# A four-layer graph network: the edges sorted by source in two lists, one gathered by pointers, one scattered as rows, and two heads added by TensorE

## What is computed

```python
# layer 0, per edge, two heads of 32
e     = sum(leaky_relu(fs[src] + fd[dst]) * attn);   alpha = softmax of e over edges with the same dst
x    += (h + sum over heads and edges of dst: softmax(fs[src] * r * alpha)) @ W1 + b1
# layer 1
x    += sum over edges of dst: h[src]
# layer 2
x    += h_self + sum over edges of dst: tensor product of h[src] with an MLP of the edge
# layer 3, four heads: here the sum runs over the edges of the SAME SRC
e     = leaky_relu(a_src[src] + a_dst[dst] + b);     att = softmax of e over edges with the same src
x    += mean over heads: sum over edges of src: att * (h @ w)[dst]
```

## Time and profile before

| | |
|---|---|
| median of 3 runs | 10985.76 us |
| the profiled execution | 10983.5 us, its span 10981.7 us |
| PE busy | 3477.1 us (32%) |
| DVE busy | 6501.1 us (59%) |
| ACT busy | 3250.7 us (30%) |
| POOL busy | 8117.5 us (74%) |
| DMA | 681.55 MB, 62 GB/s over the span |

### The profile page before, as it was taken

One profiled execution on the slowest core, in us unless ns is written; L12 is line 12 of the kernel. 1 busy time (PEld: TensorE's weight loads), 2 busy tenths in 40 slices (PEclk: granted clock), 3 DMA queues, 4 the chain that ended last, 5 costly groups with the idle time before them and its releaser, 6 DMA issues. The chain is left out here.

```text
span 10981.7 us, 94496 instructions
## 1 busy us (share of the span) xinstructions
PE 3477.1 (32%) x22119; PEld 2306.7 (21%) x22315; DVE 6501.1 (59%) x10679; ACT 3250.7 (30%) x4985; POOL 8117.5 (74%) x8449
## 2 busy tenths in 40 slices
PE   3337000005766663000000008888888200000002
PEld 2336000004655662000000003333333100000002
DVE  8995777479888884100000029999999234444442
ACT  0005433215555552111111102222222034444441
POOL 5777777777777777777777767777777677777775
PEclk6558555557888886555555558888888555555555
DMA  7212444312211211111111111111111122222222
GB/s 267 53 38 54 153 160 160 113 54 78 68 64 62 68 58 33 30 27 27 27 27 25 27 36 28 30 29 30 30 30 28 18 61 73 73 67 71 73 73 61
DMA packets 469765, 681.55 MB, mean 62 GB/s; under 512 B 270837, under 2 KB 366934, under 8 KB 431686
## 3 DMA queue, kind: packets, MB, share of 16 engines
q0 software_dynamic: 270016, 149.13, 8.6%
q10 hardware_dynamic: 67072, 346.84, 8.3%
q1 hardware_dynamic: 132614, 184.88, 5.1%
HBM read 368.75 MB, written 310.60 MB: 62 GB/s over the span
## 5 line engine op out<-in xcount | busy, mean ns | idle before, releaser
L1577 POOL DMA_INDIRECT hs<-tab_h,idx x3136 | 2975.2, 949 | 983.8 <-issue 954.8
L1163 POOL DMA_INDIRECT en<-tab_s,idx x1568 | 1483.0, 946 | 568.4 <-issue 477.4
L2145 POOL DMA_INDIRECT hs<-tab_h,idx x1568 | 1479.9, 944 | 481.9 <-issue 477.4
L1392 POOL DMA_INDIRECT by_src<-ends,pos_i x1312 | 1302.9, 993 | 405.5 <-issue 397.1
L715 DVE TENSOR_TENSOR fresh<-fresh,so_far 128x32 f32<-128x32 f32 x294 | 57.6, 196 | 1701.0 <-ACT fresh L1662 1696.5
L1799 PE MATMUL tp_ps<-w_pair,x 128*128 128x512 f32 x1568 | 908.6, 663 | 6.2 <-DVE prod_b L1939 6.2
L2031 PE MATMUL turn<-ident,both 128*33 128x128 f32 x8 | 1.9, 421 | 2108.5 <-DVEq L2061 2108.5
L947 PE MATMUL rank_ps<-place_sb,hot_t 128*128 128x98 f32 x3136 | 642.3, 316 | 5.3 <-DVE picked L1045 5.3
L584 PE MATMUL turn<-ident,tails 128*32 128x128 f32 x3 | 1.2, 396 | 2012.5 <-DMA tails<-sums 2012.5
L1662 ACT COPY fresh<-hs 128x512 f32<-128x512 f32 x98 | 99.7, 1017 | 1456.9 <-DMA hs<-tab_h,idx 1456.9
L947 PEld LDWEIGHTS rank_ps<-place_sb,hot_t 128*128 128x128 f32 x3136 | 525.0, 210 | 8.1 <-issue 3.8
(11 more groups left out here) (352 smaller groups left out, 13676.1 us busy)
## 6 DMA issues: line engine op xcount, KB each, us to landing
sums<-rows ACTq DMA_DIRECT2D x49, 2176.0 KB
sums<-rows ACTq DMA_DIRECT2D x147, 512.0 KB
hs<-tab_h,idx POOLq DMA_INDIRECT x4704
ev_rows<-zeros ACTq DMA_DIRECT2D x16, 3136.0 KB
en_rows<-en SPq DMA_DIRECT2D x49, 1024.0 KB
en_back<-en_rows ACTq DMA_DIRECT2D x49, 1024.0 KB
raw<-ev_rows ACTq DMA_DIRECT2D x49, 1024.0 KB, 4.9
en<-en_rows SPq DMA_DIRECT2D x49, 1024.0 KB
```

The source lines that it names most:

```text
L1163: pool.indirect_dma_start(en[s][:, g, :], None, tab_s0, bass.IndirectOffsetOnAxis(ap=idx[s][:, g:g + 1], axis=0)).then_inc(gathered[s], 16)
L1392: pool.indirect_dma_start(by_src, bass.IndirectOffsetOnAxis(ap=pos_i[k][:, g:g + 1], axis=0), ends[k][:, g, :], None).then_inc(sent[k], 16)
L1577: pool.indirect_dma_start(rows[k][:, g, :], None, tab_h, bass.IndirectOffsetOnAxis(ap=idx[k][:, g:g + 1], axis=0)).then_inc(gathered[k], 16)
L2145: pool.indirect_dma_start(rows[k][:, g, :], None, tab_h3, bass.IndirectOffsetOnAxis(ap=idx[k][:, g:g + 1], axis=0)).then_inc(gathered[k], 16)
```

## The change

The chunks are dealt to two lists: the even chunks to list 0, the odd ones to list 1. Each has its own counts, positions, `own_rows`, sums (`sums3`) and masks of half the length (`HCOLS`).

- Layer 0: `AHEAD` becomes 32 chunks of list 0, all ranked in the first block, whose counting makes two sets of counts. In the second block the other 17 chunks of list 0 are ranked, one a pair, in the first 17 pairs (`RANKED`); `by_src` holds only the destination and only list 0. The order in a stage changes, `en` and `r` are double-buffered, and the two heads are added by two matmuls with the identity into PSUM (`add_heads`), which scan and reuse of `z` wait for (`added`).
- Layer 1: the ranks of list 1 are made beside the gathers and kept in `pos_odd`; the block for the masks by source is gone; SP fills `hd_rows` with zeros.
- The node stage before layer 3 places `h3` at each destination's first edge in `hd_rows`.
- Layer 3 has two phases. First POOL places `a_src` for both lists, then `hd_rows` is read in order, spread by `H.scan` in the order of `dst`, and the rows of the odd chunks are scattered to `rows_src`; the masks and the sources' own values (`own_e`) are made at pairs 10 and 30. Then the attention runs over 49 chunks of list 0, gathered by pointers, and 49 of list 1, read from `rows_src` in order, alternately, each list with its own running sums.
- `mend_attention` works on both lists, and the last node stage gathers both sums and mixes them.

The excerpt follows the order of the program: ranks, layer 0 (both blocks), layer 1, the node stage before layer 3, layer 3 (POOL, ACT, DVE), the last node stage.

```diff
+            def chunk(self, r):
+                return 2 * r + (2 * self.first + self.which)
...
-        AHEAD, SENT = 16, 6
+        AHEAD, SENT = 32, 6
...
+            RANKED = PAIRS - AHEAD
+            R = Ranks(st, 0, AHEAD, iota_ps)
...
                 for t in range(SENT, AHEAD):
                     send_ahead(pool, t)
...
+                def body(p, s):
+                    K.wait(pool, "pool", posed, p + 1)
+                    for g in range(CH):
+                        pool.indirect_dma_start(by_src, bass.IndirectOffsetOnAxis(ap=pos_i[s][:, g:g + 1], axis=0),
+                                                ends[s][:, g:g + 1], None).then_inc(sent[s], 16)
...
+                turns(pool, body, end=RANKED)
...
+                def add_heads(t, k):
+                    K.wait(pe, "pe", divided, t + 1, S.scanned, t)
+                    for n in range(HEADS0):
+                        last = nc.tensor.matmul(S.message(k), ident[0:EP, 0:EP], z[k][:, :, n * FEAT:(n + 1) * FEAT].rearrange("p c f -> p f c"),
+                                                start=n == 0, stop=n == HEADS0 - 1)
+                    last.then_inc(added, 1)
...
-                    c.step(nc.vector.tensor_reduce(S.message(k), z[k][:, :, :].rearrange("p c (h f) -> p f c h", h=HEADS0), AX.X, ALU.add))
+                    S.carry(c, t, k)
+                    K.wait(dve, "dve", added, t + 1)
+                    c.join()
...
+                def send(r, k):
+                    K.wait(dve, "dve", sent[k], r * (8 * CH) - k * (8 * CH))
+                    c.link(nc.vector.tensor_copy(ends[k][:, :], dst_i[:, cols(R.chunk(r))]))
...
+                def stage(p, s, k, ranks, held):
+                    t = 2 * p + k
+                    n = p * GROUPS + 2 * k
+                    if k == 0:
+                        K.wait(dve, "dve", *held)
+                    weighed = c.mark(nc.vector.tensor_copy(weight, alpha[:, :, cols(t)].rearrange("p h c -> p c h")))
+                    K.wait(dve, "dve", added, t - 1)
+                    nc.vector.tensor_tensor(z[k][:, :, :], en[s][:, k * CH:(k + 1) * CH, :], r_in[s][:, k * CH:(k + 1) * CH, :], ALU.mult).then_inc(multiplied, 1)
+                    if ranks:
+                        if k:
+                            R.pick(dve, n - 2, s, 0)
+                        elif not first_chunk(p):
+                            R.pick(dve, n - 2, 1 - s, 2)
+                    if not first_pair(t):
+                        add_up(t - 2, k)
+                    K.wait(dve, "dve", multiplied, t + 1)
+                    z4 = heads(z[k][:, :, :])
+                    c.until(weighed)
+                    weighted = c.mark(nc.vector.tensor_tensor(z4, z4, per_head(weight), ALU.mult))
+                    if ranks:
+                        if k:
+                            R.pick(dve, n - 1, s, 1)
+                        else:
+                            if not first_chunk(p):
+                                R.pick(dve, n - 1, 1 - s, 3)
+                                send(p - 1, 1 - s)
+                            if not known_ge(p, RANKED - 1):
+                                R.hot(dve, p + 1, 1 - s)
+                    if not first_chunk(t):
+                        divide(t - 1, 1 - k)
+                    c.until(weighted)
+                    c.step(nc.vector.tensor_reduce(z_top, z4, AX.X, ALU.max))
+                    nc.vector.tensor_tensor(z4, z4, per_head(z_top), ALU.subtract).then_inc(shifted, 1)
+                def held(p, s):
...
+                turns(dve, ranked, end=RANKED, ahead=1)
...
+                alone(RANKED, RANKED % 2)
+                turns(dve, alone, first=RANKED + 1)
...
+            R = Ranks(st, 1, 0, iota_ps)
...
+                       place=lambda pool, b: pool.indirect_dma_start(hd_rows, bass.IndirectOffsetOnAxis(ap=first_dst[:, b:b + 1], axis=0),
+                                                                     h3[:, b, :], None).then_inc(hd_placed, 16))
...
+                for n in range(LISTS):
+                    for b in range(NB):
+                        pool.indirect_dma_start(own_rows[n], bass.IndirectOffsetOnAxis(ap=first_src[n][:, b:b + 1], axis=0),
+                                                a_src[:, b, :], None).then_inc(own_placed, 16)
...
+                def send(p, s):
+                    K.wait(pool, "pool", taken, p + 1)
+                    for g in range(CH):
+                        pool.indirect_dma_start(rows_src, bass.IndirectOffsetOnAxis(ap=pos2[s][:, g:g + 1], axis=0),
+                                                out_rows[s][:, g, :], None).then_inc(sent_rows[s], 16)
+                turns(pool, send, end=OWN)
+                pool.wait_ge(keyed, 1)
+                for n in range(LISTS):
+                    pool.indirect_dma_start(init[n][:, :], None, tab_a3, bass.IndirectOffsetOnAxis(ap=first_key[n][:, 0:1], axis=0)).then_inc(got_own, 16)
...
+                def body(i, s):
+                    K.wait(pool, "pool", indexed, i + 1, scored_list[0], i - 1)
+                    for g in range(CH):
+                        pool.indirect_dma_start(rows[0][s][:, g, :], None, tab_h3,
+                                                bass.IndirectOffsetOnAxis(ap=idx[s][:, g:g + 1], axis=0)).then_inc(gathered[s], 16)
+                turns(pool, body)
...
                         K.wait(act, "act", shifted, t - 1)
...
+                                       no_cont[k][:, cols(i)].unsqueeze(1).to_broadcast([EP, HEADS3, CH])).then_inc(masked, 1)
...
+                        K.wait(act, "act", shifted, t + 1, S.scanned, t - 1)
...
+                        if not first_chunk(t):
+                            S.store(act, t - 1, 1 - k, i - 1 + k)
...
+                        if k == 0:
+                            scores(i, s, 1)
+                        elif not known_ge(i, PAIRS - 1):
+                            scores(i + 1, 1 - s, 0)
+                        c.until(multiplied)
+                        dve.sem_inc(used, 1)
+                        S.scan(dve, t, k)
...
+                       gather=[(sums3[n], last_src[n], agg3[n]) for n in range(LISTS)], stores=rows_out, exps=mix)
```

More of the change, by code:

```diff
@@ L1410, in _, with alone @@
+                turns(pe, ranked, end=RANKED, ahead=1)
+                R.end_pe(pe, RANKED - 1)
+                def alone(p):
+                    for k in range(2):
+                        add_heads(2 * p + k - 1, 1 - k)
+                pairs(pe, alone, first=RANKED)
+                add_heads(last_chunk, 1)
             @block.scalar
@@ L1534, in _, with alone @@
+                send(RANKED - 1, last)
+                def alone(p, s):
+                    for k in range(2):
+                        stage(p, s, k, False, held(p, s))
+                    c.restart()
+                c.restart()
+                alone(RANKED, RANKED % 2)
+                turns(dve, alone, first=RANKED + 1)
+                K.wait(dve, "dve", added, last_chunk)
+                add_up(last_chunk - 1, 0)
+                divide(last_chunk, 1)
                 add_up(last_chunk, 1)
@@ L2159, in _, with spread @@
+                for s in range(2):
+                    index(s, s)
+                def spread(p, s):
+                    for k in range(2):
+                        H.lay(act, 2 * p + k, k, p)
+                    K.wait(act, "act", H.spread, 2 * p + 2, sent_rows[s], p * (8 * CH) - s * (8 * CH))
+                    nc.scalar.copy(pos2[s][:, :], pos_odd[:, cols(p)])
+                    nc.scalar.copy(out_rows[s][:, :, :], H.rows(1)).then_inc(taken, 1)
+                turns(act, spread)
                 act.wait_ge(started, 1)
-                own.load(act, "act", 0)
@@ L2195, in _, with spread @@
                 c = Chain(dve, chain_v)
+                dve.wait_ge(got_init, 16)
+                for ins in H.start():
+                    c.link(ins)
+                c.restart()
+                dve.sem_inc(H.freed, 1)
+                def spread(p, s):
+                    for k in range(2):
+                        H.scan(dve, c, 2 * p + k, k)
+                        if k:
+                            K.wait(dve, "dve", taken, p + 1)
+                        H.free(dve)
+                turns(dve, spread, end=MASKS)
@@ new lines, in _ @@
+                c.restart()
+                turns(dve, spread, first=MASKS, end=OWN + 10)
+                dve.wait_ge(got_own, 16 * LISTS)
+                for n in range(LISTS):
+                    c.step(nc.vector.tensor_scalar(from_before[:, :], init[n][:, 0:HEADS3], cont[n][:, 0:1], None, ALU.mult))
+                    c.step(nc.vector.tensor_tensor(own_in[n][:, 0, 0:HEADS3], own_in[n][:, 0, 0:HEADS3], from_before[:, :], ALU.add))
+                    for j in range(HEADS3):
+                        c.link(nc.vector.tensor_tensor_scan(own_e[n][:, j, :], cont[n][:, :], own_in[n][:, :, j], 0.0, ALU.mult, ALU.add))
@@ L2255, in finish, with sets_done, mix @@
```

(5 more changed lines are left out.)

909 lines of the change are left out of this document (499 added, 410 removed).

## The result

The changed kernel takes 11418.75 us (median of 4 runs, 11417.89 to 11427.37) where the kernel before took 10985.3 beside it: the ratio is 1.0396, 95% interval 1.0378 to 1.0414. Forecast were 11495 us and a range of 11320 to 11650. The profiled execution has a span of 11425.3 us against 10981.7.

A forecast was written before the change was run, and what follows sets the result against it. The kernel was taken as paced by POOL's number of indirect DMAs; stage by stage, 10981.7 + 80 - 186 + 5 + 461 + 150 = 11492, +4 for the runs' median: 11495 us, range 11320 to 11650.

The forecast's parts named there:

- second block starts: Layer 0: more ranks made ahead and a second prefix delay DVE, so the second block starts at 2425 us, +80.
- stall over: Layer 0, second block: DVE waits in `send` behind 416 ahead-scatters, standing still about 460 us, until 2978 us.
- chunk without ranks: Layer 0, second block, pairs that rank nothing: 11.75 us a chunk, 23.5 a pair, TensorE's addition of heads winning nothing.
- block two ends, against before: Layer 0's second block: stall, ranked and unranked pairs and tail end at 4159 us against 4265, -106.
- layer 3, phase (a): Layer 3, placements and scatters to the second phase's source: POOL sets the pace, 1264 us, done at 10089.
- layer 3, phase (b), pitch: Layer 3's attention loop: a chain through scan, row copy, DMA issue and `no_cont_h` sets 11.7 us a chunk.
- end: After layer 3's loop: mending two lists, 98 more gathers in the last node stage and its begin, +150 us.
- (A): Layer 0, second block: POOL is ahead of DVE's `send`, no stall; ends 460 us sooner, total 11035 us; chance 3%.
- (B): No stall, layer 3's attention loop at POOL's 20 us a pair, heads' addition covered: 10780 us, faster; 5% with mixtures.
- (E): Layer 3's attention loop: ACT's `store` done earlier, chain missing, POOL's 20 us a pair, -167: 11330 us; chance 7%.
- (D): Layer 1: added DVE work slows POOL from 1.25 to 1.298 us per DMA, 75 us: 11570 us; chance 12%.
- (C): Layer 0, second block: TensorE's fp32 additions with strided reads dominate; 3 us more cost 290 us: 11785 us; chance 6%.

The follow-up runs named there:

- the kernel with four edits: Changed kernel with a place per ranked chunk in `pos_i`/`ends`, early `no_cont_h`, `AHEAD` 24, first product in place: 0.9930, on another chip 0.9887 of the kernel before.

## Why the prediction was right

| term | predicted | measured | from |
|---|---|---|---|
| second block starts | 2425 (+80) | 2420 (+75) | POOL's first scatter, 2345.2 before |
| stall over | 2978 | 2982 | third copy into `ends`; 469.4 us in one piece (some 460) |
| ranked pair | 30 us | 30.3 | copies into `ends` |
| chunk without ranks | 11.75 us | 11.41 | starts of `z<-en,r` |
| block two ends, against before | -106 | -131 | 4287.6 to 4156.5 |
| layers 1 and 2 | +5 | +4 | |
| layer 3, phase (a) | 1264 us | 1261 | 8699.1 to 9959.7 |
| layer 3, phase (b), pitch | 11.7 us | 11.34 | 1100.2 / 97 |
| end | +150 | +146 | |
| sum of the profiled execution | 11492 | 11425 | |

The sign came from costing the change stage by stage and not by its count of DMAs: that count was right (POOL's busy time fell by 493 us) and was worth nothing, because the two stages that had fewer DMAs than before, the second block and the last layer's attention loop, each met another limit, and the first block, which had as many, grew by DVE's ranks. The stall was seen from the order of the queue alone, before any trace showed it. Its end fits to 4 us, in part by luck: the block began 5 us earlier, and the scatters ahead were 1.30 us apart, (2960.7 - 2420.0) / 416, where 1.277 was put, so they took 10 us more. Rivals (A), (B) and (E) are out by the wait of 469.4 us and the pitch of 11.34; (D) by layer 1's gathers, 1568 in the same 1970 us; and (C) by the 4.06 us from `divided` to `z`, where the sum had 4.1.

What was off: the profiled sum by 67 us, all on one side, 60 of them in two pitches. Phase (b) is 97 x 0.36 = 35 us shorter: of the chain's 11.6 us two hand-overs were mis-sized. From the last shift to the scan I put 0.4 us; it is 0.03 (10514.04 + 0.23 to 10514.30), since both are DVE's own. From the start of `no_cont_h` to `most` I put 0.4 + 0.2; it is 0.42. The rest stood as put, within 0.1 us. That accounts for the shortest turn, 11.19 us; the three others of the four add 0.13 to 0.49 us, which the sum did not have. Block two is 25 us shorter: the 10.4 us base of a chunk, in which I charged 0.7 us for three results awaited at once, was 11.4 - 1.56 = 9.8, so that a pair cost 22.8 instead of 23.5 us. The sum had a slip here, too: 10.4 and 1.5 are 11.9, not 11.75.

And one reason was right in number only. The 1.8 us for a head product came from node products that are read in order, with a clock at its 1.2 GHz level; the range for a strided read was 25.5 us a pair. At that level the stride costs nothing, and the number held. Had the clock been granted in full, the same reasoning would have said 1.0 us a product (1.96 / 2), where the strided read takes 1.8 (3.66 / 2).

## What to carry to other kernels

When one engine is the bound everywhere, taking work from it gains only down to the next limit of each stage, so find that limit stage by stage: the queue behind a small ring of buffers (count what stands ahead in the consumer's queue at the first reuse), and in a chain over engines the long copy that stands ahead of a short one in program order. They cost 468 and 125 us here, and both cures were an order or a buffer, not less work. An addition moved to an idle engine has to be covered between its start and the reuse of its operand; 1.87 us saved became 1.56 us of waiting until another product was put in between.

## What the runs showed of the hardware

- TensorE's reads of SBUF with a step of 256 bytes held an fp32 product at about 0.9 us per record of 512 columns at either level of the clock. Read in order, four records take 1.96 us at 1.00 and 3.75 at 0.50.
- A higher mean clock need not reach the products that matter: with 16 products behind each chunk's heads the mean was 0.80, but the heads, which came after 3.5 to 4.2 us without a product, still met 0.50 to 0.59. Whether products spread over the gap, with the ordered read, would remove the wait was not run.
- On two chips each kernel, the one before included, took 15.4 to 15.7 ms. The instructions compared were as long as elsewhere (the counting products have a median of 282 ns on both), but the 3136 of them took from 110 to 2973 us instead of from 112 to 881. Of the kernel with four edits on one of these chips:

```profile
L1229 PE MATMUL cnt_ps<-hot_hi,hot_lo x3136: 240/282/285, 110.3 to 2973.5; 128*128 128x98 bf16 x196
...
PEld cnt_ps L1229 <- issue: 2600.0, 193, 44.2
```

The gaps of up to 44 us between loop turns end in nothing that the profile shows. The stretch without ranks kept its pitch (11.38 us a chunk with TensorE kept busy, 11.41 in the changed kernel elsewhere). What held the engines there stays open.
